# Splitting the first key projection before the row maxima's parts, and moving its rows in two halves around the second quad's maxima

## The reference

```python
x = x + 0.5 * ffn(layernorm(x), w_gate, w_up, w_down)
x = x + attn(layernorm(x), Wq, Wk, Wv, Wo, bo)
x = x + 0.5 * ffn(layernorm(x), w_gate, w_up, w_down)

# ffn: hidden 768, integer weights times 1/127
h = silu(x @ wg.T) * (x @ wu.T);  ffn = h @ wd.T
# attn: 16 heads of 16 channels, length 512, bias by distance
scores = q @ k.T * 16 ** -0.5 - slope[h] * abs(i - j)
attn = (softmax(scores) @ v) @ Wo.T + bo
```

## Time and profile before

| | us |
|---|---|
| median of 3 runs | 805.88 |
| lowest, highest | 804.81, 812.14 |
| the profiled execution's own time | 807.18 |
| its span, first to last instruction | 805.3 |
| busy: TensorE, VectorE, ScalarE, GpSimd | 758.7, 618.4, 521.4, 450.8 |
| granted TensorE clock, mean | 0.993 |

### The profile page before, as it was taken

The page is one execution under the profiler, slowest core; times in us unless marked ns, Lnnn a source line. Parts: engine busy times, 40 slices in busy tenths (PEclk is TensorE's granted clock), DMA queues, the critical chain, the costliest instruction groups (busy, mean ns, idle before and its releaser), DMA issues.

```text
span 805.3 us, 13303 instructions
## 1 busy us (share of the span) xinstructions
PE 758.7 (94%) x4576; PEld 467.0 (58%) x4576; DVE 618.4 (77%) x1267; ACT 521.4 (65%) x1001; POOL 450.8 (56%) x550
## 2 busy tenths in 40 slices
PE   2999999999989999999999999999999997999998
PEld 1778887775443354444444454454443376988887
DVE  6698877967889968879878888879989076467763
ACT  5344444335868978878879879789788754344443
POOL 0433355425656767767766776767766555344433
PEclk9999999998999999999999999999999999999999
DMA  9440015401441650730721622522520000000001
GB/s 355 160 63 3 2 30 76 56 2 25 73 67 23 92 69 3 110 51 7 114 42 30 93 41 41 81 42 50 72 41 3 2 2 28 28 29 28 29 28 54
DMA packets 21637, 43.20 MB, mean 54 GB/s; under 512 B 3864, under 2 KB 5928, under 8 KB 21352
## 3 DMA queue, kind: packets, MB, share of 16 engines
q1 hardware_dynamic: 21544, 41.92, 28.0%
HBM read 12.02 MB, written 4.62 MB: 21 GB/s over the span
## 4 chain that ended last, share of the span: by engine, by line
PE 79%; ACT 7%; DVE 7%; issue 4%; DMA 1%; POOL 1%; DVEq 0%; ACTq 0%
PE ps L1003 73%; ACT probs L685 4%; PE ps L1066 2%; DVE row_max L881 2%; PE ps L1015 2%; DVE hid L811 1%; ACT stage L634 1%; PE ps L1071 1%; DMA q_aug<-parts 1%; DVE w_max L892 1%; ACT heads_t L669 1%; ACT xnt L652 1%; PE ps L1061 1%; DVE newton L732 1%; DMA x_sb<-x_in 0%
## 5 line engine op out<-in xcount | busy, mean ns | idle before, releaser
L881 DVE TENSOR_REDUCE row_max<-ps 128x1 f32<-128x512 f32 x512 | 326.6, 683 | 65.1 <-PE ps L1003 64.0
L685 ACT ACTIVATE probs<-ps 128x512 f32<-128x512 f32 x512 | 287.2, 607 | 49.3 <-PE ps L1003 47.6
L553 POOL TENSOR_TENSOR probs<-probs,diag 128x256 f32<-128x256 f32 x256 | 186.7, 731 | 131.7 <-ACT probs L685 130.9
L471 POOL TENSOR_TENSOR hid_r<-hid,hid_r 128x512 fp32r<-128x512 f32 x96 | 124.3, 1299 | 181.2 <-ACT hid_r L580 180.9
L1003 PE MATMUL ps<-k_aug,q_aug 60*128 60x512 f32 x512 | 191.3, 455 | 8.7 <-issue 3.8
L1003 PE MATMUL ps<-xnt,wgu_r 128*128 128x512 f32 x768 | 190.3, 402 | 7.9 <-issue 4.1
L1003 PE MATMUL ps<-q_aug,k_aug 62*128 62x512 f32 x512 | 191.6, 450 | 2.8 <-ACT probs L685 1.9
L1003 PEld LDWEIGHTS ps<-xnt,wgu_r 128*128 128x128 f32 x768 | 143.0, 190 | 46.3 <-issue 7.6
L1003 PEld LDWEIGHTS ps<-q_aug,k_aug 62*128 62x128 f32 x512 | 78.2, 186 | 120.6 <-ACT probs L685 97.6
L586 ACT ACTIVATE gated<-ps 128x512 f32<-128x512 f32 x96 | 57.4, 598 | 126.3 <-PE ps L1003 126.3
L1003 PE MATMUL ps<-probs,v_aug 128*32 128x512 f32 x1024 | 137.0, 608 | 0.1
(11 more groups left out here) (72 smaller groups left out, 672.3 us busy)
## 6 DMA issues: line engine op xcount, KB each, us to landing
q_aug<-parts SPq DMA_DIRECT2D x96, 128.0 KB, 4.6
k_aug<-parts SPq DMA_DIRECT2D x96, 128.0 KB, 4.6
x_sb<-x_in SPq DMA_DIRECT2D x8, 512.0 KB, 12.7
x_out<-x_sb SPq DMA_DIRECT2D x7, 512.0 KB, 2.6
diag<-diag_table SPq DMA_DIRECT2D x1, 2048.0 KB, 19.0
wgu_i<-w_gate_up SPq DMA_DIRECT2D x2, 768.0 KB, 6.0
w_att<-w_att SPq DMA_DIRECT2D x1, 1024.0 KB, 11.1
q_aug<-max_parts SPq DMA_DIRECT2D x64, 8.0 KB
```

Source lines behind the costliest of these rows:

```text
L471: nc.gpsimd.tensor_tensor(hid_r[:, 1, f, :], hid[:, f % 2, :], hid_r[:, 0, f, :].bitcast(F32), ALU.subtract).then_inc(s["hid_lo"], 1)
L553: nc.gpsimd.tensor_tensor(tile, tile, diag[:, kt % 2, n * QH + 2 * pair:n * QH + 2 * pair + 2, :], ALU.mult).then_inc(fixed, 1)
L685: nc.scalar.activation(probs[:, kt % 2, 2 * pair + i, :], score_bank(2 * g + i), ACT.Exp, scale=SLOPE_UNITS[pair]).then_inc(exp_done, 1)
L881: nc.vector.reduce_max(row_max[:, quad % 2, i, pair, t:t + 1], max_bank(b * MAX_TILES + tile), mybir.AxisListType.X).then_inc(s1_used, 1)
```

## The change

GpSimd's order in step (1,3) is changed: the lo part of `qk1_next` is now made right after the diagonal blocks, before the parts of `max2` (for every other fill the order is as it was). SyncE's `move_rows` takes a list of groups, and the rows of `qk1_next` are moved in two calls, group 0 ahead of `max2`'s rows and group 1 behind them. No instruction is added or removed; SyncE has one wait more, for a semaphore that is already there when it comes to it.

```diff
--- before.py
+++ after.py
@@ -394,13 +394,13 @@
                                  d_krows.rearrange("r (o t) -> r o t", o=1).to_broadcast([ROWS - ROW_BIAS, NP, L])
                                  ).then_inc(aug_in[side], 16)
 
-            def move_rows(b, name):
+            def move_rows(b, name, groups=(0, 1)):
 
                 seq, kind, part = fill_parts(b, name)
                 chunk, is_k = part // 2, part % 2
                 wait_done(sp, b, name)
                 pairs = slice(chunk * NP // CHUNKS, (chunk + 1) * NP // CHUNKS)
-                for i in range(2):
+                for i in groups:
                     for term, half in enumerate((0, 0, 1) if is_k else (0, 1, 0)):
                         at = i * GROUP + term * D
                         to = (k_aug if is_k else q_aug)[seq % 2][at:at + D, pairs, :].bitcast(F32)
@@ -431,9 +431,10 @@
                 if not last(b):
                     wait(sp, st_done, b * (2 * NQ * STEPS))
                     move_rows(b, "qk0_next")
+                    move_rows(b, "qk1_next", (0,))
                 move_max(b, "max2")
                 if not last(b):
-                    move_rows(b, "qk1_next")
+                    move_rows(b, "qk1_next", (1,))
                     move_rows(b, "qk2_next")
                 move_max(b, "max3")
                 if not last(b):
@@ -552,6 +553,9 @@
                         tile = probs[:, kt % 2, 2 * pair:2 * pair + 2, kt * P:(kt + 1) * P]
                         nc.gpsimd.tensor_tensor(tile, tile, diag[:, kt % 2, n * QH + 2 * pair:n * QH + 2 * pair + 2, :],
                                                 ALU.mult).then_inc(fixed, 1)
+                        rows_first = name == "qk1_next"
+                        if rows_first:
+                            take(b, name)
                         if s == 3 and FILLS[n, 4] in fills_of(b):
                             split_max(b, FILLS[n, 4])
                         if (n, s) == (0, 3):
@@ -561,7 +565,7 @@
                                 add_bo(b + 1, (s // 2,))
                             if (n, s) in PLACE_AT:
                                 place_v(b + 1, PLACE_AT[n, s])
-                        if name:
+                        if name and not rows_first:
                             take(b, name)
 
             turns(pool, turn)
```

## The result

The changed kernel took 815.66 us (median of 22 runs, 810.27 to 823.05); the kernel before, run beside it, 809.62 (median of 22, 804.30 to 815.87). The ratio is 1.0084 with a 95% interval of 1.0057 to 1.0111: slower, by about 6.8 us, under the 1% that the prediction had called no change. One run of the changed kernel, 823.05, is over 1.5% above its fastest and is left out of the ratio; the quotient of the two medians is 1.0075. Its own time, 807.1, was put on the earlier median of 805.88; what was forecast is +1.2, and the size is more than five times that.

What follows compares the result with a forecast made beforehand. TensorE's work plus its stops was taken to bound each turn: +8.28 at (2,0), -7.09 at (2,3), turn 6 nothing, together +1.2 on the median 805.88 gives 807.1 us; range 800.2 to 810.5.

Steps and rivals of the forecast that it cites:

- The stop at (2,3): TensorE's wait before tile 64 for the next sequence's key rows, turns 0 to 5, would go: -7.09 us.
- the way the queue would run: SyncE's queue: three key transfers, two of the maxima, three key transfers, in one piece of some 5 us.
- the stop at (2,0): New TensorE wait for the maxima's rows at the first score, 1.38 us in each of turns 0 to 5: +8.28 us.
- Turn 6: New stop taken as hidden by TensorE's wait for VectorE in (2,1), costing nothing; 1.38 us more if that cover is gone.
- its upper end, 810.5: Top of the range: turn 6 at full price (+1.38), a slow turn-0 key transfer (+1.25), under a microsecond of scatter.
- turns longer by more than 0.6 us each: Sign of being wrong: attention turns that shorten or lengthen by more than 0.6 us each.
- A: The forecast itself, 807.1 us, with a new stop of 1.2 to 1.5 us before the first score of (2,0); chance 0.50.
- D: Maxima's rows share engines with group 1's first transfer, landing 1.04 us later; stop 2.42 at (2,0), 814.3 us; chance 0.05.
- B: Maxima's small transfers not held up: stop of 0.37 us at (2,0), old stop gone, 801.0 us; chance 0.27.
- C: Last key row still lands 5.4 us after its issue, pair not held up; both stops stand at 0.37, 804.3 us; chance 0.13.
- the lower end: Maxima's rows land at 276.50 in turn 1 with nothing ahead: stop of 0.37 us at (2,0), sum -4.9 us.
- The estimate from two engines' share: Maxima's pair waits only for two engines' part of group 0, so the sum falls between -4.9 and +1.2 us.

Runs made afterwards that it cites:

- Experiment 1: Changed kernel with seven unread 128x512 products on TensorE ahead of its wait for the second quad's maxima, turns 0 to 6: 808.04 us, ratio 1.0008 to the kernel before.
- Experiment 7: Changed kernel with SyncE's new order but GpSimd making the maxima's parts first, as in the kernel before: 832.92 us, ratio 1.0287 to the kernel before.
- experiment 8: Changed kernel with all six key transfers ahead of the maxima's pair: 838.26 us in two runs, ratio 1.0360 to the kernel before.
- experiment 6: Changed kernel with the maxima's pair issued by ScalarE on its own queue, SyncE's six key transfers in a row: 833.01 us, ratio 1.0294 to the kernel before.
- experiment 5: Changed kernel with only 128 of 512 columns of group 0 ahead of the maxima's pair, the rest behind: 813.67 us, ratio 1.0059 to the kernel before.
- experiment 11: Kernel before with four unread 128x512 products on TensorE ahead of tile 64 at (2,3), turns 0 to 6: 802.29 us, ratio 0.9925 to the kernel before.
- experiment 12: Changed kernel with one key transfer ahead of the pair, five behind, and two unread products ahead of tile 64: 804.68 us, ratio 0.9937 to the kernel before.
- experiments 2 to 12: Eleven kernels varying transfer order, bytes, queue, GpSimd's order or unread TensorE products, on the changed kernel or the one before: ratios 0.9922 to 1.0360 to the kernel before.

## Why the prediction was wrong, point by point

**The stop at (2,3) goes, all 7.09 us of it: right.** So was the way the queue would run, and that GpSimd's idle time would be filled.

**The step that failed is the size of the stop at (2,0), and with it the sum.** The prediction took 1.38 in each of six turns, 8.28 in all, from the third key transfer's landing, 5.47 after the first issue. That landing was right. The pair came 0.57 behind it, 6.04 after the first issue; TensorE came 4.23 after that issue, where 4.09 was forecast, which took 0.14 back: 1.38 + 0.57 - 0.14 = 1.81 in turn 1. Turns 0 and 2 to 6 are alike but for turn 3, where the stop is 2.59: there the pair comes 6.82 after the first issue, though the three key transfers land as in turn 1, and why stays open. Turns 0 to 5 make 11.5 instead of 8.28.

**Turn 6 was not hidden.** The prediction costed the stop there at nothing, since VectorE was what TensorE waited for the earlier trace rows. The stop is 1.76, and nothing hides it: VectorE catches up and the wait for it of 0.24 in (2,1) is gone, but one of 0.28 stands later in the turn, at 583.84. The turn is 2.3 longer (58.33 for 56.04), with its fall. With this stop they are 13.26, and the sum of stops is +6.2 instead of +1.2.

**The clock had no term at all.** The prediction moved a stop from one place to another and priced both by their length. The stops grew from about 1.0 to about 1.8, and five of seven then brought a fall, 0.5 to 1.3 us each and 4.8 together in the profiled execution. Experiment 1 shows that it is the stop's doing. This is in no row of the kernel before, where no fall followed a stop in the turns, but the range had no room for it either: its upper end, 810.5, was the stop's own bounds.

**The sizes against the runs.** The two profiles differ by 11.0 us in the turns, the runs by 6.8. The stops' +6.2 would make nearly all of that by themselves. The falls count for less in the runs than in the two profiles, since the kernel before has some too: its granted clock is 0.991 on the mean over the 93 runs beside the experiments, the changed kernel's is 0.987. As time at half the clock that is 14.5 against 21.8 us, some two falls more and not five; at 1.33 us for one of 3.4 us this is an estimate of +2.9. Together that would be +9, the upper end of the measured interval (4.6 to 9.0). Where in the program the runs have their falls is in no record, so the share of each stays an estimate.

**The prediction's own signs of being wrong.** It named turns longer by more than 0.6 us each, and five of seven are, by 1.65 to 2.29. It gave a stop of 1.2 to 1.5 for A and of over 2 for D; six of the seven lie between the two.

**The rivals.** D, the slower one, came near by its time (814.3) and partly by luck: it had the pair 1.04 behind group 0, which was 0.57, and no clock in it. Its mechanism, that the pair shares with the transfers behind it, was not tested and is not excluded. Experiment 7 leaves group 1 in its place. In experiment 8, with nothing issued behind the pair for over 2 us, it is there with the last transfer ahead and not 0.57 behind it; in experiment 6, with the last of the six right behind it, it is 1.5 later. Both fit D's mechanism. B, not held up, is excluded by the rows after (a stop of 1.81 in turn 1, not 0.37); experiment 5 shows what B takes, few bytes ahead. C is excluded by the rows after: no stop is left before tile 64, and the last key transfer lands 4.2 after its own issue instead of 5.4. The rule of the Trainium skill that was weighed against the lower end ("Queues, rings and completion order") gave the right side: the trace agrees, in turn 1 the pair was there 0.57 after the third transfer, and in no turn before 5.87 after the first issue. The estimate from two engines' share, that the pair would be there between the two ends, did not come true: it was beyond the upper one.

## What to carry to other kernels

A small transfer that somebody waits for is as late as the bytes of the large ones that are under way, on whatever queue it is issued; before anything is put ahead of it, find its slack (here 1.4 us) and count the transfers that fit into it (here one, which won 0.65% in the runs, though the stops explain only a third of it, where three lost 0.84%). And a stop of TensorE is not priced by its length alone: look at the granted clock behind it. When a stop can't be removed, products that nobody reads may be cheaper than the idle time (experiment 1: 4.3 us in the seven turns), but they don't have to be (experiment 11: 1.4 us more there; experiment 12: no gain). And before a gain is put down to the place that was edited, compare the stretches that were not: in experiment 11 most of it lay in another layer.

## What the runs showed of the hardware

**Stops and falls of the clock.** Over thirteen traces, those of the kernel before, the changed one and experiments 2 to 12 (stops of under 0.45 left out), the stops at (2,0) and before tile 64 and the clock after each: of 30 stops of 0.45 to 1.25 us none was followed by a fall; of 25 of 1.39 to 2.59 us, 14 were; of 22 of 2.98 us and more, all were. In the changed kernel the fall is to 0.50 for about 3.4 us; in four turns it begins 1.3 to 1.6 us after the stop's end, in turn 5 at the stop's end. Other falls lie elsewhere: at 193 to 201 in the kernel before, behind the stop of 3.01 in its second feed-forward layer, and 20 us long in turn 7 of experiment 12. Between 1.4 and 2.6 us length alone doesn't decide: 1.42 and 1.53 brought one, 2.30 and 2.59 did not. The Trainium skill ("TensorE: Matmul & The Clock Gate", section "HAM oscillation — how this bites in real kernels") describes waits for a DMA after which TensorE starts each round at the low clock; the trace agrees in kind.

**A transfer of 8 KB** is there about 2 us after its issue alone, 3.35, 3.6 and 4.0 behind two, three and six transfers of 128 KB on its own queue, and 5.4 after its issue from another queue while six of them are under way. The issue is that of the pair's second transfer, the landing is where TensorE goes on.
